# Depthwise and omni convolutions on 112-row tiles without a gap, band blocks packed, row sums taken channel by channel

## The chip, the cores and the metric

The kernel runs on one core of one Trainium2 chip. The metric is the device time of one execution in microseconds (us). Engines: PE is TensorE, with PEld for its weight loads; DVE is VectorE; ACT is ScalarE; POOL is GpSimd; SP only issues DMAs here, as ACT also does. Before the change, three runs gave 5991.86, 6002.13 and 6011.43 us, a median of 6002.13 us.

## The reference

The input x is 16 images of 192 channels of 56 by 56 pixels, float32. Two blocks follow each other.

```
# block 1
x_pw = bn(einsum('bchw,oc->bohw', x, pw_w)) + x
out  = bn(dwconv(x_pw, 13x13)) + bn(x_pw * dw1_w)
y    = gelu(out)                                  # erf form
# block 2, tok = y as tokens of 192 channels
xi   = omni(ln(tok) * ln1_g + ln1_b)              # a0*x + a1*dw1x1 + a2*dw3x3 + a3*dw5x5
k, v, r = xi @ wk.T, xi @ wv.T, sigmoid(xi @ wr.T)
v    = wkv along rows, then along columns         # two scans over 3136 tokens
tok += gamma1 * ((r * v) @ wo.T)
xf   = omni(ln(tok) * ln2_g + ln2_b)
tok += gamma2 * (sigmoid(xf @ wr.T) * (square(relu(xf @ wk.T)) @ wv.T))
```

What the change touches are the three depthwise convolutions (13x13 once, 5x5 twice) and the sums over channels that the layer norms need.

## The kernel before

`build` (L1658) runs blocks one after the other, with all engines meeting between them: `prepare` (weights), `pointwise` (the 1x1 convolution), `depthwise` (13x13), `norm_scales`, `omni` (5x5), `attention`, `norm_scales`, `omni`, `feed_forward`. Intermediate images go through scratch tensors in device memory. I call the three convolution blocks dw13, omni1 and omni2.

**How a depthwise convolution becomes matmuls.** A channel's 16 images are cut into 28 pairs of image rows. A pair of rows lies on the partitions: row 0 on partitions 0 to 55, row 1 above. A convolution over rows and columns is then a few products with banded matrices: for each distance d between the pair read and the pair written there is one band matrix, and the moving operand is all pairs of all images shifted by d (up to 16 x 28 = 448 columns). dw13 has d from -3 to 3, omni from -1 to 1. Each product is three matmuls (L87 to L89), since operands are split into a rounded high part and a rest: high x high, high x rest, rest x high. That makes 21 matmuls for a channel of dw13, 9 for a channel of omni.

**The gap.** The two rows of a pair stand at PITCH = 62 partitions from each other, with 6 zero partitions (56 to 61) between them in tiles of PXP = 118 partitions; PXC = 112 is the count without the gap. A channel's bands are a matrix with `cols` columns (862 for 13x13, 366 for 5x5) of which the product for d reads the 118 columns from 124 * (dmax ± d). In omni the first gap partition carries the layer norm's bias: its row of the bands is the "edge" row, and its row in the input is a constant (made from a row of -1 in the table of means, L775). In dw13 the input and the bands already use 112 partitions (`parts` = PXC), but outputs, and the bands' columns, still have the gap.

**dw13 (`depthwise`, L362).** Groups of 8 channels, 24 groups, two buffers. For each channel:
- ACT rounds the bands (L529, 112x862) and the input, which it turns from image order into pair order (L531); it does so 3 channels ahead, into 4 slots
- POOL subtracts: rest of the bands (L418), rest of the input (L488)
- PE does the 21 matmuls; ACT applies Gelu with a bias from PSUM into the group's output (L545)

After a group's 8 channels DVE makes the sums for the layer norm: it sums the 8 channels (`tensor_reduce`, L507), adds to the running sum (L509), squares the group (L510), sums (L512) and adds (L514). SP loads the input and bands of the group after next (L430, L441); ACT stores the group (L548). At the start DVE clears both band tiles (L495) before SP may load.

**omni (L561).** The same, with these differences: DVE scales the input by the table of inverse deviations (L681, 4 channels at a time), writing it in pair order, then subtracts the table of means (L687); both tables lie in PSUM. DVE also makes the rest of the bands (L693), POOL the rest of the input (L661), ACT the two roundings (L721, L723) and the copy out of PSUM (L734). At the start DVE clears four whole tiles (L667, L668). The loads of the group after next are issued by SP when the input has been scaled, and when the last band of the group has been split. `copy_pairs` (L118) makes every load and store that crosses the gap of two DMAs of 56 partitions:

```
    for r in range(2):
        tile, rest = slice(r * PITCH, r * PITCH + W), r * W
```

`norm_scales` (L751) turns the sums into the two tables; its last step is a DMA that writes the row of -1.

Of the kernel before, what the change touches and what calls it, by code (L numbers as in the profile page):

```python
# [117 lines left out]
def copy_pairs(eng, to, of, signal):  # L118


    for r in range(2):
        tile, rest = slice(r * PITCH, r * PITCH + W), r * W
        part = []
        for ap in (to, of):
            dims = [list(d) for d in ap.ap]
            if dims[0][1] == PXP:
                part.append(ap[tile])
            else:
                part.append(bass.AP(ap.tensor, ap.offset + rest * dims[0][0], [[dims[0][0], W]] + dims[1:]))
        eng.dma_start(part[0], part[1]).then_inc(signal, 16)  # L130
# [231 lines left out]
def depthwise(nc, B, name, src, parts, k, f_d, dst, bias_d, stats, flipped=False):  # L362

    dmax, centre, length, cols = band(k)
    N = B * PJ
    assert N <= 512
    with ExitStack() as ctx:
        m = Mem(nc, ctx)
        wt = [m.sb(f"{name}_band{u}", [PXP, G, cols]) for u in range(2)]
        raw = [m.sb(f"{name}_in{u}", [PXP, B, G, PJ]) for u in range(2)]
        z = raw
        out = [m.sb(f"{name}_out{u}", [PXP, B, G, PJ]) for u in range(2)]  # L380
# [9 lines left out]
        zeroed = m.sem(f"{name}_bands_zeroed")  # L390
# [5 lines left out]
        out_read = m.sem(f"{name}_output_summed")  # L396
        sq = m.sb(f"{name}_squares", [PXP, B, G, PJ])
        part = [m.sb(f"{name}_part{n}", [PXP, B, PJ]) for n in range(2)]
        reduced = m.sem(f"{name}_group_reduced")
        summed = m.sem(f"{name}_sums_updated")  # L400
        block = ctx.enter_context(nc.Block())
        flat = lambda t: t[:, :, :].rearrange("p a b -> p (a b)")
        by_pair = lambda ap: ap.rearrange("p b j -> p j b")
        IN = 32
        BASE = 2 * G
        step_in = PITCH if parts == PXP else W
# [6 lines left out]

        def rest_of_band(eng, i, n):
            u, cc, _, _ = channel(i, n)
            p = [q[0:parts, :] for q in wp[n % SLOTS]]
            eng.wait_ge(rounded_done, i * (4 * G) + (2 * n + 1))
            eng.tensor_tensor(rounded(p[1]), wt[u][0:parts, cc, :], p[0], ALU.subtract).then_inc(band_split, 1)  # L418

        @block.sync  # L420
        def _(sp):
# [1334 lines left out]
```

## Time and profile before

| | us |
|---|---|
| runs, median of 3 | 6002.13 |
| the profiled execution, its own time | 6008.11 |
| its span in the profile | 6006.3 |
| PE busy | 4937.5 |
| DVE busy | 4211.5 |
| ACT busy | 3702.6 |
| POOL busy | 3425.7 |

The profiled execution has 6 us over the median. The granted clock of PE has a mean of 0.929. Busy PE counts pipelined matmuls in full, so a busy PE isn't PE at its peak. Stages, from the first and last instruction of each: dw13 runs from about 379 to 1213, omni1 from 1222 to about 1690, omni2 from 3737 to about 4190, with the attention in between and the feed-forward behind.

### The profile page before, as it was taken

To read this page: it belongs to the slowest core of one execution; us is meant where nothing else is said; L and a number is where in the kernel's file an instruction comes from. 1 tells how busy PE (TensorE), PEld (TensorE's weight loads), DVE (VectorE), ACT (ScalarE), POOL (GpSimd) and SP (SyncE) were. 2 spreads that over 40 slices of the span, in tenths; PEclk is the share of its full clock that TensorE was granted. 3 is DMA by queue.
4 is the path that set the end of the run, shared out by engine and by line. 5 is a ranking of instruction groups with operands and counts; after the bars stand their busy time and mean duration, and the time that the engine had idled before them with its cause. 6 is when DMAs were issued, how large, how long until landed. Compare 5 with 4: busy or idle time off the path is not lost. (4 is left out here: it accounts for less than half of the span.)

```text
span 6006.3 us, 77285 instructions
## 1 busy us (share of the span) xinstructions
PE 4937.5 (82%) x23504; PEld 3954.3 (66%) x23504; DVE 4211.5 (70%) x5193; ACT 3702.6 (62%) x6950; POOL 3425.7 (57%) x2796
## 2 busy tenths in 40 slices
PE   5969999958866766767667673788899999999999
PEld 5969999847632443433334332676788888888888
DVE  4427777789849898888888885897555555555555
ACT  0016666545557888888888884565565665656565
POOL 0019999835549687777777872454444444444444
PEclk9979999979988988888889886999999999999999
DMA  6977777578840223213212122887422322322320
GB/s 170 264 187 197 193 196 205 148 185 255 245 104 11 68 52 76 65 43 88 54 44 65 44 65 56 233 268 226 105 69 54 82 60 56 86 56 54 88 54 24
DMA packets 389868, 689.60 MB, mean 115 GB/s; under 512 B 22399, under 2 KB 347986, under 8 KB 370194
## 3 DMA queue, kind: packets, MB, share of 16 engines
q1 hardware_dynamic: 335184, 529.89, 36.6%
q10 hardware_dynamic: 54386, 156.21, 7.3%
q8 instruction: 130, 2.13, 0.2%
q14 instruction: 168, 1.38, 0.1%
HBM read 452.17 MB, written 233.87 MB: 114 GB/s over the span
## 5 line engine op out<-in xcount | busy, mean ns | idle before, releaser
L1543 POOL TENSOR_TENSOR hidden_part<-hidden_whole,hidden_part 128x448 fp32r<-128x448 f32 x672 | 751.5, 1154 | 1025.9 <-ACT hidden_part L1508 1025.7
L661 POOL TENSOR_TENSOR omni_in_part<-omni_norm,omni_in_part 118x448 fp32r<-118x448 f32 x384 | 466.0, 1215 | 555.5 <-ACT omni_in_part L723 539.7
L1412 PE MATMUL f_out_ps<-hidden_part,ffn_wv_parts 128*128 128x448 f32 (+1 forms) x3360 | 720.8, 370 | 0.7 <-POOL hidden_part L1543 0.7
L418 POOL TENSOR_TENSOR dw_band_part<-dw_band,dw_band_part 112x862 fp32r<-112x862 f32 x192 | 438.7, 2285 | 470.6 <-ACT dw_band_part L529 470.5
L1412 PEld LDWEIGHTS f_out_ps<-hidden_part,ffn_wv_parts 128*128 128x128 f32 (+1 forms) x3360 | 578.1, 177 | 103.7 <-POOL hidden_part L1543 35.1
L87 PE MATMUL omni_ps<-omni_in_part,omni_band_part 118*118 118x432 f32 (+1 forms) x1152 | 435.7, 378 | 236.2 <-DVE omni_band_part L693 218.4
L1217 POOL TENSOR_TENSOR input_times_v<-input_factor,v_all 128x448 f32<-128x448 f32 x336 | 419.6, 1249 | 362.8 <-ACT input_factor L1110 343.3
L1586 DVE TENSOR_SCALAR hidden_whole<-f_hid_ps 128x448 f32<-128x448 f32 x672 | 417.6, 622 | 250.5 <-POOL hidden_part L1543 155.9
L1039 PE MATMUL proj_ps<-mixT_low,kvr_weights_low 128*128 128x448 f32 x672 | 354.0, 611 | 203.9 <-ACT k_all L1101 174.1
L87 PE MATMUL dw_ps<-dw_in_part,dw_band_part 112*118 112x432 f32 (+3 forms) x1344 | 473.7, 352 | 57.4 <-POOL dw_in_part L488 57.4
L1041 PE MATMUL proj_ps<-mixT_ends,kvr_weights_ends 128*128 128x448 f32 x1008 | 515.3, 595 | 0.0
L89 PE MATMUL dw_ps<-dw_in_part,dw_band_part 112*118 112x432 f32 (+3 forms) x1344 | 476.4, 354 | 0.0
L88 PE MATMUL dw_ps<-dw_in_part,dw_band_part 112*118 112x432 f32 (+3 forms) x1344 | 474.0, 353 | 0.0
L529 ACT ACTIVATE dw_band_part<-dw_band 112x862 fp32r<-112x862 f32 x192 | 176.2, 918 | 411.9 <-DMA dw_band<-flat 398.4
L89 PE MATMUL omni_ps<-omni_in_part,omni_band_part 118*118 118x432 f32 (+1 forms) x1152 | 419.5, 364 | 0.0
L88 PE MATMUL omni_ps<-omni_in_part,omni_band_part 118*118 118x432 f32 (+1 forms) x1152 | 418.9, 364 | 0.0
L1224 POOL TENSOR_TENSOR v_all<-input_times_v,input_factor 128x448 f32<-128x448 f32 x336 | 385.0, 1146 | 58.1 <-ACT input_factor L1126 55.7
L87 PEld LDWEIGHTS omni_ps<-omni_in_part,omni_band_part 118*118 118x118 f32 x1152 | 209.0, 181 | 312.0 <-DVE omni_band_part L693 270.9
L1055 PE MATMUL out_ps<-attention_out_weights,r_all 128*112 128x193 f32 x896 | 246.0, 359 | 200.5 <-DVE residual_pairs L1302 170.3
L1508 ACT ACTIVATE hidden_part<-hidden_whole 128x448 fp32r<-128x448 f32 x672 | 388.9, 579 | 21.3
L1412 PE MATMUL f_hid_ps<-ffn_mixT_part,ffn_wk_high 128*128 128x448 f32 x1344 | 396.2, 376 | 5.3 <-DVE hidden_whole L1586 5.3
L721 ACT ACTIVATE omni_band_part<-omni_band 118x366 fp32r<-118x366 f32 x384 | 194.0, 505 | 304.6 <-DMA omni_band<-edge_att 148.9
(183 smaller groups left out, 13650.6 us busy)
## 6 DMA issues: line engine op xcount, KB each, us to landing
dw_band<-flat SPq DMA_DIRECT2D x48, 1508.5 KB
xin<-x SPq DMA_DIRECT2D x16, 2352.0 KB, 13.1
x_pointwise<-xp ACTq DMA_DIRECT2D x16, 2352.0 KB, 18.9
dw_in<-x_pointwise SPq DMA_DIRECT2D x24, 1568.0 KB
y_gelu<-dw_out ACTq DMA_DIRECT2D x48, 784.0 KB
omni_in<-y_gelu SPq DMA_DIRECT2D x48, 784.0 KB
att_mix<-omni_out ACTq DMA_DIRECT2D x48, 784.0 KB
residual_pairs<-y_gelu SPq DMA_DIRECT2D x16, 2352.0 KB, 11.9
```

The costliest lines, as they stand in the source:

```text
L87: pe.matmul(bank, w_hi, x_hi, start=start, stop=False)
L88: pe.matmul(bank, w_hi, x_lo, start=False, stop=False)
L89: return pe.matmul(bank, w_lo, x_hi, start=False, stop=stop)
L418: eng.tensor_tensor(rounded(p[1]), wt[u][0:parts, cc, :], p[0], ALU.subtract).then_inc(band_split, 1)
L661: pool.tensor_tensor(rounded(p[1][:, :, :]), z[u][:, cc], p[0][:, :, :], ALU.subtract).then_inc(in_split, 1)
L1041: pe.matmul(to[:, 0:TC], keep.w_end[:, o, part * 128:(part + 1) * 128], x_end[:, t, :], start=False, stop=True).then_inc(bank_ready, 1)
L1217: pool.tensor_tensor(grid(EV[unit.slot % 2]), grid(E[unit.slot]), part_of(vS, unit), ALU.mult).then_inc(ev_done, 1)
L1224: pool.tensor_tensor(part_of(vS, unit), grid(EV[unit.slot % 2]), grid(E[unit.slot]), ALU.mult).then_inc(wkv_done, 1)
L1412: return pe.matmul(bank, rounded(w), rounded(x), start=start, stop=stop)
L1508: act.activation(rounded(kk[n % 2][0][:, h, :]), whole[h % KW][:, :], ACT.Copy).then_inc(kh_ready, 1)
L1543: pool.tensor_tensor(rounded(kk[n % 2][1][:, h, :]), whole[h % KW][:, :], kk[n % 2][0][:, h, :], ALU.subtract).then_inc(kl_ready, 1)
L1586: dve.tensor_scalar_max(whole[h % KW][:, :], hidden_bank(n, h)[:, 0:TC], 0.0).then_inc(relu_done, 1)
```

## The change

- Tiles of the three convolutions have 112 partitions, the two rows next to each other, and outputs have no gap. Matmuls of dw13 go from 118 to 112 output rows, those of omni from 118 x 118 to 113 x 112.
- The band tiles in memory keep their 862 and 366 columns, but the parts are packed: `band_blocks` reads 14 blocks (dw13) or 6 (omni) of 56 columns at a pitch of 62, so that a part has 784 or 336 columns.
- `load_band_rows` doesn't load the 56 columns or the 62 that are always zero for a row of the pair; POOL clears these margins, once. The whole-tile memsets are gone. dw13's loads wait for POOL's four memsets; omni's first input doesn't wait at all.
- Loads and stores of images are one DMA of 112 partitions in place of two of 56. Band loads are still two of 56.
- dw13's sums are made by channel: square, add to the sum, add the square to its sum, all three on DVE for every channel, in place of two reduces, a square and two adds for a group.
- omni keeps its input in image order from the load to the matmul. The parts have one zero pair ahead and one behind each image, so that a shift by d is a shift of the window: all 9 matmuls have 448 columns, read as 16 pieces of 28. The bias row is partition 112, set to 1 by a DMA of ones.
- `norm_scales` no longer writes the row of -1, and its memsets and paired DMAs are gone.

```
+def band_blocks(ap, count):
+    return free(ap, [[PITCH, count], [1, W]])
+def blocks(ap):
+    return ap.rearrange("p (n w) -> p n w", w=W)
+def load_band_rows(eng, wt, f_d, at, length, cols, signal):
+    for r, (lo, hi) in enumerate(((PITCH, cols), (0, cols - W))):
+        eng.dma_start(wt[r * W:(r + 1) * W, :, lo:hi],
+                      dram(f_d, at + (PITCH * r + lo), [[1, W], [length, G], [1, hi - lo]])).then_inc(signal, 16)
...
 depthwise, PE
-                        at = 2 * PITCH * (dmax - d if flipped else dmax + d)
-                        mm = split_matmul(pe, ps[cc][0:PXP, lo * B:hi * B],
+                        at = PXC * (dmax - d)
+                        mm = split_matmul(pe, ps[cc][0:PXC, lo * B:hi * B],
...
 depthwise, POOL
+            for u in range(2):
+                for margin in (slice(0, PITCH), slice(cols - W, cols)):
+                    pool.memset(wt[u][:, :, margin], 0.0).then_inc(zeroed, 1)
...
-                    rest_of_band(pool, i, n)
+                    p = wp[n % SLOTS]
+                    pool.wait_ge(rounded_done, i * (4 * G) + (2 * n + 1))
+                    pool.tensor_tensor(rounded(blocks(p[1][:, :])), band_blocks(wt[u][:, cc, :], BLOCKS),
+                                       blocks(p[0][:, :]), ALU.subtract).then_inc(band_split, 1)
...
 depthwise, DVE
-                dve.memset(wt[u][:, :, :], 0.0).then_inc(zeroed, 1)
...
-                    dve.tensor_reduce(part[0][:, :, :], by_pixel(out[u]), AX_X, ALU.add).then_inc(reduced, 1)
-                    dve.tensor_add(s1[:, :], s1[:, :], flat(part[0])).then_inc(summed, 1)
-                    dve.tensor_mul(sq[:, :, :, :], out[u][:, :, :, :], out[u][:, :, :, :]).then_inc(out_read, 1)
-                    dve.tensor_reduce(part[1][:, :, :], by_pixel(sq), AX_X, ALU.add).then_inc(reduced, 1)
-                    dve.tensor_add(s2[:, :], s2[:, :], flat(part[1])).then_inc(summed, 1)
+                for n in range(2 * G):
+                    u, cc, number, _ = channel(i, n)
+                    o = out[u][:, :, cc, :]
+                    dve.wait_ge(ps_free, number + G)
+                    dve.wait_ge(squares_summed, number)
+                    dve.tensor_mul(sq[:, :, :], o, o).then_inc(squared, 1)
+                    dve.wait_ge(summed, number + G)
+                    dve.tensor_add(s1, s1, o).then_inc(summed, 1)
+                    dve.wait_ge(squared, number + (G + 1))
+                    dve.tensor_add(s2, s2, sq[:, :, :]).then_inc(squares_summed, 1)
...
 depthwise and omni, ACT, at a group's end
-                        copy_pairs(act, pair_group(dst, B, i * 2 + u),
-                                   out[u][:, :, :, :].rearrange("p b c j -> p (b c j)"), stored[u])
+                        act.dma_start(pair_group(dst, B, i * 2 + u),
+                                      out[u][:, :, :, :].rearrange("p b c j -> p (b c j)")).then_inc(stored[u], 16)
...
 omni
+        z = [m.sb(f"{name}_norm{u}", [ROWS, B, G, PJ]) for u in range(2)]
+        wp = [[m.sb(f"{name}_band{s}_part{n}", [ROWS, BLOCKS * W]) for n in range(2)] for s in range(SLOTS)]
+        zp = [[m.sb(f"{name}_in{s}_part{n}", [ROWS, B, 1 + PJ + 1]) for n in range(2)] for s in range(SLOTS)]
...
 omni, SP
+            load_input(place(0), 0)
+            for u in range(2):
+                sp.dma_start(z[u][PXC:ROWS, :, :, :].rearrange("p b c j -> p (b c j)"), ones
+                             ).then_inc(ones_loaded, 16)
             sp.wait_ge(zeroed, 4)
-            for u in range(2):
-                load_input(place(u), u)
-                load_bands(place(u), u)
+            load_bands(place(0), 0)
+            load_input(place(1), 1)
+            load_bands(place(1), 1)
...
 omni, PE
-                        mm = split_matmul(pe, ps[n % NB][0:PXP, lo * B:hi * B],
-                                          [x[:, at:at + PXP] for x in wp[n % SLOTS]],
-                                          [flat(x)[:, (lo + d) * B:(hi + d) * B] for x in zp[n % SLOTS]],
+                        at = PXC * (dmax + d)
+                        mm = split_matmul(pe, by_image(ps[n % NB][0:PXC, 0:N]),
+                                          [x[:, at:at + PXC] for x in wp[n % SLOTS]],
+                                          [x[:, :, 1 + d:1 + d + PJ] for x in zp[n % SLOTS]],
...
 omni, POOL: margins as in depthwise, and the pads of the parts
+            for s in range(SLOTS):
+                for x in zp[s]:
+                    pool.memset(x[:, :, :], 0.0).then_inc(padded, 1)
...
 omni, DVE
-                dve.memset(wt[u][:, :, :], 0.0).then_inc(zeroed, 1)
-                dve.memset(raw[u][:, :, :, :], 0.0).then_inc(zeroed, 1)
...
-                dve.tensor_mul(by_image(z[u][:, part]), raw[u][:, :, part, :], free(rs_ps, [[PJ, B], [0, H], [1, PJ]])
-                               ).then_inc(scaled, 1)
+                dve.tensor_mul(z[u][0:PXC, :, part, :], raw[u][:, :, part, :], of_table(rs_ps)).then_inc(scaled, 1)
...
 norm_scales, SP
-            sp.wait_ge(step, 5)
-            sp.dma_start(s1[W:W + 1, :], minus_one).then_inc(gap_set, 16)
-            sp.wait_ge(gap_set, 16)
```

## Rows read from the trace of the kernel before

**Rows 1.** Busy time of each engine by stretch: pointwise, dw13, omni1, omni2; (x) instructions, then PE clock, DMA share, GB/s.
```profile
120.00:240.00 120.00, 120.00 (x740) 120.00 (x739) 51.22 (x92) 0.00 (x0) 0.00 (x0) 1.00 1.01 268
...
800.00:1200.00 400.00, 394.20 (x2070) 369.56 (x2069) 294.51 (x63) 244.45 (x300) 361.54 (x194) 1.00 0.68 180
...
1295.00:1691.00 396.00, 334.77 (x1572) 278.16 (x1570) 339.17 (x256) 235.40 (x520) 213.05 (x173) 0.99 0.85 241
...
3790.00:4190.00 400.00, 349.50 (x1656) 292.87 (x1656) 356.95 (x272) 252.55 (x547) 217.62 (x182) 1.00 0.85 250
```

**Rows 2.** Timeline of ACT in omni1, two copies out of PSUM that each waited for PE.
```profile
1441.91 0.55 ACT L734 ACTIVATE omni_out<-omni_ps 118x448 f32<-118x448 f32 x1 [0.38 <-PE omni_ps L89]
...
1443.70 0.55 ACT L734 ACTIVATE omni_out<-omni_ps 118x448 f32<-118x448 f32 x1 [0.38 <-PE omni_ps L89]
```

**Rows 3.** Waits from 1295 to 1691: engine, line, waited for, us in total, times, longest.
```profile
ACT omni_band_part L721 <- DMA omni_band<-edge_att: 108.3, 20, 7.4
```

**Rows 4.** Groups of instructions, DVE in omni1 and omni2.
```profile
L681 DVE TENSOR_TENSOR omni_norm<-omni_in,omni_scales 118x1792 f32<-118x1792 f32 x96 | 318.0, 3315 | 23.9 <-issue 20.1 <-DMA omni_in<-y_gelu 2.4 <-DMA omni_in<-tok 1.3
...
L693 DVE TENSOR_TENSOR omni_band_part<-omni_band,omni_band_part 118x366 fp32r<-118x366 f32 x384 | 295.7, 789 | 83.3 <-ACT omni_band_part L721 82.8
...
L687 DVE TENSOR_TENSOR omni_norm<-omni_norm,omni_scales 118x1792 f32<-118x1792 f32 x96 | 192.9, 2011 | 0.0
```

**Rows 5.** DMA queues from 1300 to 1690: packets, MB, share of 16 engines.
```profile
q1 hardware_dynamic: 21445, 58.70, 61.0%
q10 hardware_dynamic: 3064, 35.10, 24.2%
```

**Rows 6.** Timeline from the end of dw13 to the first matmul of omni1.
```profile
1194.90 0.77 ACTq L130 DMA_DIRECT2D y_gelu<-dw_out  x2
...
1212.54 0.62 DVE L514 TENSOR_TENSOR y_square_sum<-y_square_sum,dw_part 118x448 f32<-118x448 f32 x1
...
1222.24 2.50 DVE L667 MEMSET omni_band<- 118x2928 f32 x1 [2.35 <-PEq L637]
...
1235.31 0.77 SPq L130 DMA_DIRECT2D omni_in<-y_gelu  x2
...
1246.40 6.14 DVE L681 TENSOR_TENSOR omni_norm<-omni_in,omni_scales 118x1792 f32<-118x1792 f32 x2 [10.08 <-issue]
...
1257.76 0.72 PE L87 MATMUL omni_ps<-omni_in_part,omni_band_part 118*118 118x448 f32 x1 [63.56 <-DVE omni_band_part L693]
```

**Rows 7.** Timeline at the start of dw13.
```profile
378.87 5.80 DVE L495 MEMSET dw_band<- 118x6896 f32 x1 [12.32 <-issue]
386.06 5.80 DVE L495 MEMSET dw_band<- 118x6896 f32 x1 [1.39 <-issue]
...
418.92 0.92 ACT L529 ACTIVATE dw_band_part<-dw_band 112x862 fp32r<-112x862 f32 x1 [398.40 <-DMA dw_band<-flat]
```

**Rows 8.** Groups of instructions, POOL in dw13: busy us, mean ns, idle before.
```profile
L418 POOL TENSOR_TENSOR dw_band_part<-dw_band,dw_band_part 112x862 fp32r<-112x862 f32 x192 | 438.7, 2285 | 470.6 <-ACT dw_band_part L529 470.5
...
L488 POOL TENSOR_TENSOR dw_in_part<-dw_in,dw_in_part 112x448 fp32r<-112x448 f32 x192 | 292.4, 1523 | 0.0
```

**Rows 9.** Timeline of DVE and POOL in dw13: start us, duration us, instruction.
```profile
705.48 0.90 DVE L514 TENSOR_TENSOR y_square_sum<-y_square_sum,dw_part 118x448 f32<-118x448 f32 x1
...
727.38 3.88 DVE L510 TENSOR_TENSOR dw_squares<-dw_out 118x3584 f32<-118x3584 f32 x1
...
705.86 1.79 POOL L488 TENSOR_TENSOR dw_in_part<-dw_in,dw_in_part 112x448 fp32r<-112x448 f32 x1
707.60 2.08 POOL L418 TENSOR_TENSOR dw_band_part<-dw_band,dw_band_part 112x862 fp32r<-112x862 f32 x1
709.62 1.42 POOL L488 TENSOR_TENSOR dw_in_part<-dw_in,dw_in_part 112x448 fp32r<-112x448 f32 x1
710.99 1.73 POOL L418 TENSOR_TENSOR dw_band_part<-dw_band,dw_band_part 112x862 fp32r<-112x862 f32 x1
...
727.77 5.41 POOL L418 TENSOR_TENSOR dw_band_part<-dw_band,dw_band_part 112x862 fp32r<-112x862 f32 x1 [0.80 <-ACT dw_band_part L529]
```

More of the change, by code:

```diff
@@ L557, in _, with omni @@
             for u in range(2):
-                act.wait_ge(stored[u], 32 * (NG // 2 + 1))
-def omni(nc, B, name, src, f_d, s_d, dst, rs, ms):
+                act.wait_ge(stored[u], 16 * (NG // 2 + 1))
+def omni(nc, B, name, src, f_d, s_d, ones, dst, rs, ms):
     dmax, _, length, cols = band(K5)
+    BLOCKS = 2 * (2 * dmax + 1)
     N = B * PJ
+    ROWS = PXC + 1
     assert N <= 512
@@ L595, in omni @@
         BASE = 2 * G
-        W_LOADS, IN_LOADS = 48, 32
-        flat = lambda t: t[:, :, :].rearrange("p j b -> p (j b)")
+        W_LOADS, IN_LOADS = 48, 16
+        by_image = lambda ap: ap.rearrange("p (b j) -> p b j", j=PJ)
+        inner = lambda t: t[:, :, 1:1 + PJ]
+        of_table = lambda ap: free(ap, [[PJ, B], [0, H], [1, PJ]])
         def channel(i, n):
@@ L655, in _ @@
         def _(pool):
+            for u in range(2):
+                for margin in (slice(0, PITCH), slice(cols - W, cols)):
+                    pool.memset(wt[u][0:PXC, :, margin], 0.0).then_inc(zeroed, 1)
+            for s in range(SLOTS):
+                for x in zp[s]:
+                    pool.memset(x[:, :, :], 0.0).then_inc(padded, 1)
+            pool.wait_ge(padded, 2 * SLOTS)
             with pool.Fori(0, NG // 2) as i:
@@ L802, in _ @@
             act.activation(s2[:, :], s2[:, :], ACT.Sqrt).then_inc(root, 1)
-def transposed(bank, reverse=False):
-    s = -1 if reverse else 1
-    return free(bank[0:CT, :], [[PXP, JC], [s * PITCH, 2], [s, W]], PXP - 1 if reverse else 0)
 def turned(bank, rows):
@@ L1685, in build @@
                 mi = Mem(nc, inner)
-                s1, s2 = mi.sb("y_sum", [PXP, B * PJ]), mi.sb("y_square_sum", [PXP, B * PJ])
-                depthwise(nc, B, "dw13", xpw_d, PXC, K13, f13_d, y_d, bias_d, (s1, s2), flipped=True)
-                norm_scales(nc, "ln1", s1, s2, ins["minus_one"], kept_d=sy_d)
-                omni(nc, B, "omni1", y_d, f5a_d, sa_d, mixa_d, s2, s1)
+                s1, s2 = mi.sb("y_sum", [PXC, B * PJ]), mi.sb("y_square_sum", [PXC, B * PJ])
+                depthwise(nc, B, "dw13", xpw_d, K13, f13_d, y_d, bias_d, (s1, s2))
+                norm_scales(nc, "ln1", s1, s2, kept_d=sy_d)
+                omni(nc, B, "omni1", y_d, f5a_d, sa_d, ins["ones"], mixa_d, s2, s1)
             attention(nc, B, keep, mixa_d, y_d, sy_d, tok_d, s1_d, s2_d)
@@ L1692, in build @@
                 mi = Mem(nc, inner)
-                s1, s2 = mi.sb("t_sum", [PXP, B * PJ]), mi.sb("t_square_sum", [PXP, B * PJ])
-                norm_scales(nc, "ln2", s1, s2, ins["minus_one"], s1_d, s2_d)
-                omni(nc, B, "omni2", tok_d, f5f_d, sf_d, mixf_d, s2, s1)
+                s1, s2 = mi.sb("t_sum", [PXC, B * PJ]), mi.sb("t_square_sum", [PXC, B * PJ])
+                norm_scales(nc, "ln2", s1, s2, s1_d, s2_d)
+                omni(nc, B, "omni2", tok_d, f5f_d, sf_d, ins["ones"], mixf_d, s2, s1)
         feed_forward(nc, B, ins, keep, mixf_d, tok_d, out)
@@ L1730, in layout @@
         "ident": np.eye(PXP, dtype=np.float32),
-        "minus_one": np.full((1, x.shape[0] * PJ), -1.0, np.float32),
+        "ones": np.ones((1, x.shape[0] * G * PJ), np.float32),
         "pw_wt": t(l0("pw_w")),
```

197 lines of the change are left out of this document (77 added, 120 removed).

## The prediction

> **What bounds the kernel now.** I read the busy times by stage first [rows 1], since a mean over the span mixes stages. In dw13 PE issues without a pause: 2070 matmuls in 394.2 us of work, so a channel's 21 take 4.00 us. POOL is busy 361.5 of 400 us there, the second limit and not far off. In both omni stages PE is busy 85 to 87%, DVE 86 to 89%, and the DMA share stands at 0.85, whereas in the pointwise stage it reached 1.01. A channel takes 396 / 1572 x 9 = 2.27 us in omni1 and 400 / 1656 x 9 = 2.17 us in omni2, so a group of 8 takes 18.1 and 17.4 us. Where PE is fed, two channels follow each other in 1443.70 - 1441.91 = 1.79 us, 14.3 us for a group [rows 2]. So omni waits. The waits say for what: ACT stood 108 us of 396 waiting for bands to land, at 20 group starts [rows 3]. DVE is no better placed: 8 x 0.789 + 2 x 3.315 + 2 x 2.011 = 17.0 us for a group [rows 4], some of it waiting that the durations hold.
>
> Why 0.85 is a full DMA: per group of omni the output is 1.61 MB, the input the same, the bands 1.31 MB. From 1300 to 1690 the output queue used 24.2% of 16 x 390 us for 35.1 MB = 21.9 groups, 69 engine-us each; the other queue 61.0% for 58.7 MB, 20.0 groups, 190 each, of which 69 are input and 121 bands [rows 5]. The sum 259 over 16 engines is 16.2 us, over 14 it is 18.5, and the measured period is 18.1. Pointwise has transfers of 96 and 112 partitions and a share near 1; omni's large ones all have 56, and 0.85 is near 14/16 [rows 1]. I take it that a 56-partition transfer uses 14 engines. The Trainium skill ("DMA: Bandwidth & Descriptors", why a DMA increments its semaphore by 16) says that the number of engines is the largest up to 16 that divides the slowest dimension, 14 for 56 and 16 for 112; the share agrees.
>
> **omni, steady state.** Bytes: bands shrink from 366 to 304 and 310 columns, 0.839 of before, 121 to 102 engine-us. Images move on 16 engines instead of 14; bands stay at 56 rows. Busiest engines: (69 + 69) / 16 + 102 / 14 = 15.9 us, against 18.5 by the same sum before. PE: now 9 x 448 = 4032 columns where it had 3936, so 1.79 becomes 1.83 us, 14.7 for a group. DVE: L681 wrote pair order at 3.3 us; in image order it should cost what L687 does, 2.0, so 8 x 0.79 + 4 x 2.01 = 14.4. ACT and POOL keep their work, in pieces of 28 elements. The slowest of these is the DMA at 15.9, where its model read 18.5 for a measured 18.1 and 17.4; I take 15.8 for both. Gain: 24 x (18.1 - 15.8) + 24 x (17.4 - 15.8) = 93 us. At best PE bounds: 24 x (3.4 + 2.7) = 146. If engines aren't what limits and only the bytes count (239.5 / 259 = 0.925), 24 x (1.4 + 1.3) = 65.
>
> **omni, start.** DVE's four memsets stand between 1222.24 and the first load at 1235.31; the first matmul comes at 1257.76 [rows 6]. Now the first load goes out at once, and the row of -1, whose transfer shows as 2.35 us idle ahead of 1222.24, is gone, so at about 1220.3. Landing takes at most the 11.1 us from 1235.31 to 1246.40, and from the first scaling to the first matmul it was 11.4 us, now 2 x 1.3 less: first matmul at 1220.3 + 11.1 + 8.8 = 1240.2, a gain of 17.6. POOL's 12 memsets (448 to 496 columns) are not in the trace: as fast as DVE's 5.80 us for 6896 columns [rows 7] they take 0.4 us each, at POOL's 1.52 us for 448 [rows 8] some 1.6. Even then, 19 us in all, ACT starts at 1240 and the gain is 14. I take 18 for each omni, 36 together.
>
> **dw13, start.** Two memsets hold the loads back from 378.87 to 391.86 [rows 7]. Four of POOL's, 1.6 to 6.5 us by the same two prices, take their place; 3 is nearest to a memset's own price. That is 10 us, and of the 27.1 us until 418.92 the bands, 6.8% fewer bytes, give 1. Gain 11.
>
> **dw13, end.** After the last Gelu DVE works from 1194.9 to 1213.16 [rows 6]. With sums by channel three operations of 0.62 us are left, and the stage ends with the last store, issued at 1194.90: 69 / 16 = 4.3 us of transfer and some us of latency, about 1202. Gain 11 (8 to 16).
>
> **dw13, steady state: the price of the change.** PE's work doesn't shrink: output rows of a matmul are not its columns. But DVE now makes 3 operations a channel, each with both inputs in SBUF, beside POOL's two. The timeline shows what that costs [rows 9]: L510 ran from 727.38 to 731.26, and POOL's L418, issued at 727.77, took 5.41 us where it takes 2.08 or 1.73 alone. L514 beside L488 made it 1.79 instead of 1.42: 0.37 us lost to POOL for one operation of 448 columns. POOL alone needs 3.39 us for a channel (707.60 to 710.99) at the slower of its two band times and 0.35 less at the other, 3.2 on average; with 784 columns instead of 862 (9% of 1.9) 3.05. Adding 3 x 0.37 gives 4.16 us against PE's 4.00: POOL and DVE together become the limit, by 0.16 x 192 = 31 us. DVE itself isn't late: ACT waits for its sums only when an output buffer comes round, 8 channels later. PE's waits on the new limit are short, so its clock should stay at 1.00.
> Bounds: below nothing, since PE's 4.00 doesn't move. Above, POOL loses the 0.62 us that an add takes alone [rows 6]: 3.05 + 1.86 = 4.91. Or its band subtraction in 14 pieces runs at the per-element time of L488, which reads transposed: 1.42 x 784 / 448 = 2.48 in place of 1.73, again 4.91 with 0.37. Either is 175 us. I take 31, as L418 stays contiguous in runs of 56 and the 0.37 is measured.
> The Trainium skill ("SBUF — State Buffer", the engine ports) says that a DVE operation with two SBUF inputs and a POOL operation reading SBUF exclude each other for the whole instruction. The row of L510 agrees; that of L514 shows less than the whole, 0.37 of 0.62. By the page's rule the stage would take 4.91 us a channel.
>
> **Sum.** -11 - 11 + 31 - 36 - 93 = -120 us. Everything else (pointwise, attention, feed-forward) is untouched. The profiled execution took 6008.1 us, so 5888; it has 6 over the median of 6002.1, against which it is 5882.
>
> **Rivals.**
> - *The port doesn't bind* (0.20): what DVE takes falls into POOL's idle tenth, the channel stays at 4.00: 31 us more gained, 5851. For it speaks that durations on POOL are rough; against it, that POOL is busy nine tenths already.
> - *omni stays where it is* (0.12): the rate at which bands and images come isn't set by engines or bytes, and DVE's gain is hidden behind it. -120 + 93 = -27, 5975. Against it: at equal bytes the model gives the period within 7%.
> - *Whole exclusion in dw13* (0.12), the slower end: every add holds POOL for 0.62 us, 4.91 us a channel, +175 in place of +31: +24, 6026. It decides from 0.88 us a channel on, since the rest gives 151 and slower means 18 us. For it the stretch of L418, against it that of L514.
> - *The shifted windows don't do what they say* (0.04): PE reads 28-column pieces at half the rate. Then a channel of omni takes 3.67 us, a group 29.4: 24 x (11.3 + 12.0) = 559 slower, not 93 faster, about 6530. No row shows a matmul that reads in pieces, so nothing but the contiguous rate speaks against it.
>
> **Numbers.** The forecast has 0.52. About 0.3% (18 us) is what a measurement can tell from no change. Forecast, free port and three quarters of the flat omni are faster: 0.81. Slower: the whole exclusion up to its milder part, and the slow windows: 0.13. The rest, 0.06, is no change. Range: the low end has the free port and nearly PE's bound in omni, -11 - 11 - 36 - 146 = -204, about 5805; the high end takes in the flat omni with some more of the port's price, 5990.
>
> **What would show it.** Right: L418 near 1.7 to 2.1 us when undisturbed, PE in dw13 with short waits for POOL at 4.1 to 4.2 us a channel, DVE's adds often over 1 us; L681 at 2.0; DMA share in omni up, the wait for bands down, a group at 15.8; first matmul of omni some 20 us after the norm. Wrong: dw13's channel over 4.5 or at 4.00; L681 still at 3.3; omni's matmuls longer at a clock of 1.00; omni's group over 17.

## The result, and the profile after

The changed kernel takes 5950.9 us (median of 4, 5947.2 to 5954.1) against 5997.0 of the kernel before on the same chip (median of 4, 5991.2 to 6011.4): a ratio of 0.992, 95% interval 0.9906 to 0.9933. It is 46 us faster where 120 were forecast. The profiled executions have spans of 5948.0 and 6006.3 us, 58.3 apart; the stages below are read from these two. "Norm" is the block `norm_scales`.

| stretch | before | after | difference | forecast |
|---|---|---|---|---|
| dw13, first matmul at | 423.4 | 407.0 | -16 | -11 |
| dw13, first to last matmul | 770.5 | 828.1 | +58 | +31 |
| dw13, last Gelu to norm | 19.3 | 17.9 | -1 | -11 |
| omni1 and omni2, norm to first matmul | 44.3, 47.8 | 26.0, 29.2 | -37 | -36 |
| omni1, first matmul to last store's issue | 430.4 | 395.0 | -35 | -55 |
| omni2, the same | 417.4 | 398.1 | -19 | -38 |

The starts came nearly as forecast. Two things did not: dw13 lost nearly twice what was set for it and gave almost nothing back at its end, and omni's steady state gained little more than half.

**dw13.** The stretch of [rows 1] and, under it, what ACT waited for from 407 to 1330 (engine, line, waited for: us in total, times, longest):
```profile
800.00:1200.00 400.00, 376.59 (x1901) 340.71 (x1900) 393.77 (x271) 220.01 (x283) 347.50 (x183) 0.96 0.64 168
```
```profile
ACT dw_out L526 <- PE dw_ps L89: 190.3, 112, 3.4
ACT dw_out L526 <- DVE y_sum L494: 86.9, 11, 10.3
ACT L526 <- DVE y_sum L494: 69.6, 8, 8.7
```
DVE went from 295 to 394 us of 400: it is the engine that is hardly ever idle, and ACT's first Gelu of a group (L526), which writes an output buffer, waited 156 us for its sums. The forecast had looked for PE waiting on POOL. The timeline of DVE and POOL shows how, in the stretch of [rows 9]:
```profile
698.21 2.12 POOL L470 TENSOR_TENSOR dw_band_part<-dw_band,dw_band_part 112x784 fp32r<-112x784 f32 x1
698.65 2.16 DVE L494 TENSOR_TENSOR y_sum<-y_sum,dw_out 112x448 f32<-112x448 f32 x1
700.29 1.79 POOL L474 TENSOR_TENSOR dw_in_part<-dw_in,dw_in_part 112x448 fp32r<-112x448 f32 x1
700.73 1.84 DVE L496 TENSOR_TENSOR y_square_sum<-y_square_sum,dw_squares 112x448 f32<-112x448 f32 x1
702.04 2.12 POOL L470 TENSOR_TENSOR dw_band_part<-dw_band,dw_band_part 112x784 fp32r<-112x784 f32 x1
702.68 1.97 DVE L492 TENSOR_TENSOR dw_squares<-dw_out 112x448 f32<-112x448 f32 x1
...
719.06 0.62 DVE L494 TENSOR_TENSOR y_sum<-y_sum,dw_out 112x448 f32<-112x448 f32 x1
719.60 0.62 DVE L496 TENSOR_TENSOR y_square_sum<-y_square_sum,dw_squares 112x448 f32<-112x448 f32 x1
719.85 0.64 ACT L526 ACTIVATE dw_out<-dw_ps,dw_cols 112x448 f32<-112x448 f32 x1 [8.30 <-DVE y_sum L494]
721.31 2.25 POOL L470 TENSOR_TENSOR dw_band_part<-dw_band,dw_band_part 112x784 fp32r<-112x784 f32 x1 [3.92 <-ACT dw_band_part L511]
```
In the first six lines one DVE start stands between each two POOL starts; over the whole stage that holds for 341 of the 354 pairs of POOL operations that follow each other without a pause. POOL's operations are 0.40 longer than alone (2.12 for 1.72, 1.79 for some 1.40; the values alone are e3's, below), so it gets through a channel in 702.04 - 698.21 = 3.83 us, faster than PE's 4.00. DVE gets two turns in that time and needs three. It falls behind by most of an operation a channel, until ACT stands still at a group's start, POOL runs dry (3.92 us), and DVE catches up at 719.60 - 719.06 = 0.54 us each.

**omni.** Stretches in both omni stages, columns as in [rows 1]; then PE's matmuls on either kernel's tile (ns, least/median/most), before first; then DVE's and POOL's groups in omni1.
```profile
1316.00:1596.00 280.00, 268.18 (x1226) 213.98 (x1225) 206.59 (x205) 182.78 (x410) 215.81 (x136) 1.00 0.98 263
3760.00:4040.00 280.00, 266.86 (x1219) 212.66 (x1218) 204.63 (x202) 179.30 (x403) 213.71 (x135) 1.00 0.97 262
```
```profile
L87 PE MATMUL omni_ps<-omni_in_part,omni_band_part x1152: 353/362/724, 1257.8 to 4187.4; 118*118 118x448 f32 x192
```
```profile
L87 PE MATMUL omni_ps<-omni_in_part,omni_band_part x1152: 373/377/684, 1279.3 to 4135.2; 113*112 113x448 f32 x192
```
```profile
L655 POOL TENSOR_TENSOR omni_in_part<-omni_norm,omni_in_part 113x448 fp32r<-113x448 f32 x192 | 298.9, 1567 | 104.4 <-ACT omni_in_part L714 102.9
...
L681 DVE TENSOR_TENSOR omni_band_part<-omni_band,omni_band_part 113x336 fp32r<-113x336 f32 x191 | 112.6, 591 | 99.2 <-ACT omni_band_part L711 99.0
L670 DVE TENSOR_TENSOR omni_norm<-omni_in,omni_scales 112x1792 f32<-112x1792 f32 x46 | 92.6, 2013 | 4.4 <-DMA omni_in<-y_gelu 4.3
```
The scaling fell to 2.01 us as forecast [rows 4]. The DMA share is 0.98 and 0.97, where before had 0.89 in the same two stretches (0.85 over the whole stages), which looks as if more engines took part, as forecast; yet the rate rose by 4 to 5% only, to 262 and 263 GB/s from before's 253 and 250 (before's second stretch begins 11 us ahead of omni2's first matmul):
```profile
1316.00:1596.00 280.00, 237.26 (x1108) 196.54 (x1107) 251.26 (x187) 164.69 (x364) 149.14 (x122) 0.99 0.89 253
3760.00:4040.00 280.00, 233.76 (x1091) 195.57 (x1092) 254.01 (x188) 169.15 (x369) 148.50 (x124) 0.96 0.89 250
```
A group takes 395.0 / 24 = 16.5 us, and ACT still waited for bands 79.5 us in omni1. Matmuls of 448 columns in pieces of 28 follow each other every 0.215 us (e6, below), where the forecast had 0.203.

### The profile page after: what moved, and what is told of

Its sections match the earlier page's. It is cut to its first block and busy times, and to the rows that moved or that the text cites. A ratio compares the mean times of both kernels' runs of the same rounds, so it can differ in the third digit from the quotient of the medians.

```text
span 5948.0 us, 77644 instructions
## 1 busy us (share of the span) xinstructions
PE 4981.9 (84%) x23504; PEld 3940.7 (66%) x23504; DVE 4253.6 (72%) x5637; ACT 3670.0 (62%) x6950; POOL 3588.9 (60%) x2824
## 5 line engine op out<-in xcount | busy, mean ns | idle before, releaser
L655 POOL TENSOR_TENSOR omni_in_part<-omni_norm,omni_in_part 113x448 fp32r<-113x448 f32 x384 | 602.9, 1581 | 206.8 <-ACT omni_in_part L714 204.1
L1564 DVE TENSOR_SCALAR hidden_whole<-f_hid_ps 128x448 f32<-128x448 f32 x672 | 417.4, 622 | 250.0 <-POOL hidden_part L1521 157.4
L87 PE MATMUL dw_ps<-dw_in_part,dw_band_part 112*112 112x432 f32 (+3 forms) x1344 | 484.5, 361 | 77.9 <-POOL dw_in_part L474 41.3
L87 PE MATMUL omni_ps<-omni_in_part,omni_band_part 113*112 113x448 f32 x1152 | 439.7, 382 | 118.7 <-POOL omni_in_part L655 87.9
L88 PE MATMUL dw_ps<-dw_in_part,dw_band_part 112*112 112x432 f32 (+3 forms) x1344 | 483.2, 360 | 0.0
L89 PE MATMUL dw_ps<-dw_in_part,dw_band_part 112*112 112x432 f32 (+3 forms) x1344 | 479.7, 357 | 0.0
L470 POOL TENSOR_TENSOR dw_band_part<-dw_band,dw_band_part 112x784 fp32r<-112x784 f32 x192 | 400.6, 2087 | 123.5 <-ACT dw_band_part L511 122.8
L88 PE MATMUL omni_ps<-omni_in_part,omni_band_part 113*112 113x448 f32 x1152 | 437.4, 380 | 0.0
L89 PE MATMUL omni_ps<-omni_in_part,omni_band_part 113*112 113x448 f32 x1152 | 437.0, 379 | 0.0
L511 ACT ACTIVATE dw_band_part<-dw_band 112x784 fp32r<-112x784 f32 x192 | 164.5, 857 | 390.1 <-DMA dw_band<-flat 382.4
L1484 ACT ACTIVATE hidden_whole<-hidden_whole 128x448 f32<-128x448 f32 x672 | 379.2, 564 | 0.9 <-DVE hidden_whole L1564 0.3
L1019 PEld LDWEIGHTS proj_ps<-mixT_ends,kvr_weights_ends 128*128 128x128 f32 x1008 | 192.9, 205 | 270.3 <-issue 270.3
```

Of the source, the lines that this page charges most:

```text
L87: pe.matmul(bank, w_hi, x_hi, start=start, stop=False)
L88: pe.matmul(bank, w_hi, x_lo, start=False, stop=False)
L89: return pe.matmul(bank, w_lo, x_hi, start=False, stop=stop)
L470: pool.tensor_tensor(rounded(blocks(p[1][:, :])), band_blocks(wt[u][:, cc, :], BLOCKS), blocks(p[0][:, :]), ALU.subtract).then_inc(band_sp ...
L655: pool.tensor_tensor(rounded(inner(p[1])), z[u][:, :, cc, :], inner(p[0]), ALU.subtract).then_inc(in_split, 1)
L1019: pe.matmul(to[:, 0:TC], keep.w_end[:, o, part * 128:(part + 1) * 128], x_end[:, t, :], start=False, stop=True).then_inc(bank_ready, 1)
```

## The experiments

Theory for dw13 (**turns**): while both have work, DVE gets one operation for each of POOL's; what doesn't fit runs when POOL is idle, at 0.54 us each. With k DVE operations a channel, a channel takes 3.83 + 0.54 (k - 2), at least PE's 4.00. Rivals: each DVE operation simply adds its 0.40 us to POOL's 3.12 (3.12 + 0.40 k, "port time" in the texts below); DVE holds POOL for its whole 0.62 us; the gapless tiles themselves are slower. The texts of e1 and e2 give the sum of port times as the theory and the whole 0.62 as its rival; turns as a formula came out of their results, so its agreement with them below was no forecast, and e10 is its only test ahead of a result. All times are from the first to the last matmul of dw13 unless said. Runs before e11 are single ones beside 5995.7 (e1 to e4), 5998.4 (e5 to e8) and 5999.4 (e9, e10; a median of nine) of the kernel before.

**e1, two operations a channel.**
```diff
-                    dve.tensor_add(s2, s2, sq[:, :, :]).then_inc(squares_summed, 1)
```


> The changed kernel with the add into s2 left out (the sums of squares stay 0): DVE has two operations a channel in dw13 instead of three. After took 828 us from dw13's first to its last matmul, 4.31 a channel. Theory (port time adds up): POOL's two subtractions take 3.12 us alone (1.72 + 1.40), each DVE operation with two SBUF inputs adds 0.40, a channel takes max(4.00, 3.12 + 0.40 k), so 4.00 for k = 2 (3.92 is hidden behind PE), the stretch 774 us, the kernel about 54 us shorter than after, and ACT no longer waits for DVE's sums. Rival 1 (DVE holds POOL for its whole 0.62 us): 3.12 + 1.24 = 4.36, no change. Rival 2 (PE or ACT is slower on the gapless tiles, the sums have no part in it): 4.31, no change.

5878.1 us; 767.7, 4.00 a channel. ACT waited for no sum, the norm began 8.1 us after the last Gelu instead of 17.9.

**e2, four operations.**
```diff
+                    dve.tensor_add(extra[:, :, :], sq[:, :, :], sq[:, :, :]).then_inc(extra_done, 1)
```


> The changed kernel with one more DVE operation a channel in dw13, sq + sq into a tile that nobody reads: four instead of three. Theory (port time adds up): 3.12 + 4 x 0.40 = 4.72 us a channel, 906 us from first to last matmul, 78 more than after. Rival 1 (whole 0.62 us each): 0.62 more a channel, 4.93, 119 us more. Rival 2 (the sums have no part in it): 4.31, no change.

6055.5 us; 927.6, and 24.2 us from the last Gelu to the norm. DVE and POOL, the same view as above:
```profile
1289.72 1.79 POOL L476 TENSOR_TENSOR dw_in_part<-dw_in,dw_in_part 112x448 fp32r<-112x448 f32 x1
1290.16 1.83 DVE L500 TENSOR_TENSOR y_square_sum<-y_square_sum,dw_squares 112x448 f32<-112x448 f32 x1
1291.46 2.13 POOL L472 TENSOR_TENSOR dw_band_part<-dw_band,dw_band_part 112x784 fp32r<-112x784 f32 x1
1291.91 2.16 DVE L502 TENSOR_TENSOR dw_extra<-dw_squares 112x448 f32<-112x448 f32 x1
...
1295.27 2.15 POOL L472 TENSOR_TENSOR dw_band_part<-dw_band,dw_band_part 112x784 fp32r<-112x784 f32 x1
```
POOL still needs 1295.27 - 1291.46 = 3.81 us a channel: the fourth operation costs POOL nothing while both run. Counting what the end of the stage takes over e1's 8.1 us to the stretch, a channel takes (828.1 + 9.8) / 192 = 4.36 us with three operations and (927.6 + 16.1) / 192 = 4.92 with four; turns give 4.37 and 4.91. Added port times give 4.32 and 4.72, and the whole 0.62 us gives 4.98 and 5.60. The sum of port times falls by e2 alone, the whole 0.62 us by both, and slower tiles by e1's 4.00.

**e3, the sums in PSUM.** Four banks for the convolution instead of eight, two for the sums.
```diff
-            s1, s2 = [by_image(s[:, :]) for s in stats]
+            s1, s2 = [by_image(s[0:PXC, 0:N]) for s in sums]
...
+            for total, s in zip(sums, stats):
+                dve.tensor_copy(s[:, :], total[0:PXC, 0:N]).then_inc(kept, 1)
```


> The changed kernel with the two sums of dw13 kept in two PSUM banks (the convolution has four banks instead of eight) and copied to SBUF at the end: of DVE's three operations a channel only the square reads two tiles from SBUF. Theory (only two-input SBUF operations take POOL's time): 3.12 + 0.40 = 3.52, hidden behind PE: 4.00 a channel, 774 us; DVE keeps up, so the norm begins 8 to 10 us after the last Gelu instead of 17.9; 54 + 8 = 62 us shorter than after. Rival (adds with one input in PSUM stretch POOL as well, as the scaling in omni seems to): 4.31, no change. Rival 2 (four banks are too few): PE waits on bank_free, over 4.00 without POOL being busy.

5883.6 us; 768.8, and 8.0 us to the norm. Groups of dw13:
```profile
L473 POOL TENSOR_TENSOR dw_band_part<-dw_band,dw_band_part 112x784 fp32r<-112x784 f32 x191 | 342.6, 1794 | 153.2 <-ACT dw_band_part L519 153.0
L477 POOL TENSOR_TENSOR dw_in_part<-dw_in,dw_in_part 112x448 fp32r<-112x448 f32 x191 | 272.5, 1427 | 0.0
...
L495 DVE TENSOR_TENSOR dw_squares<-dw_out 112x448 f32<-112x448 f32 x192 | 148.2, 772 | 447.2 <-ACT dw_out L534 447.2
L497 DVE TENSOR_TENSOR dw_sum<-dw_sum,dw_out 112x448 f32<-112x448 f32 x192 | 119.6, 623 | 0.0
```
The same add that took 1.56 us on the mean beside POOL (after's L494) takes 0.62 with its sum in PSUM, whatever POOL does, and POOL is back near its own 1.72 and 1.40. Four banks are enough.

**e4, sums by group on gapless tiles.** DVE's part of the kernel before, on 112 partitions.
```diff
-                    dve.tensor_add(s1, s1, o).then_inc(summed, 1)
...
+                    dve.tensor_reduce(part[0][:, :, :], by_pixel(out[u]), AX_X, ALU.add).then_inc(cleared, 1)
...
```


> The changed kernel with the sums of dw13 by group as before (a reduction over 8 channels, an add, a square, a reduction, an add), on 112 partitions. Theory: dw13 from first to last matmul back at 4.00 a channel, 774 us, 54 less than after, and the end of the stage takes some 19 us from the last Gelu to the norm. Rival 2 (the gapless tiles themselves slow dw13): stays at 4.31.

5895.2 us; 767.6, and 19.2 us to the norm. So the sums by channel are the whole loss in dw13: without them the rest of the change is worth 100 us (5995.7 - 5895.2, single runs). The same trace shows where the rule of turns ends. Here DVE's additions stand alone between long reductions, and two of the 48 got no turn as long as POOL had work; the longer one waited past seven POOL starts at 1.38 to 1.74 us each, until POOL paused for 0.98 us:
```profile
942.73 11.23 DVE L496 TENSOR_TENSOR y_square_sum<-y_square_sum,dw_part 112x448 f32<-112x448 f32 x1
942.91 1.40 POOL L475 TENSOR_TENSOR dw_in_part<-dw_in,dw_in_part 112x448 fp32r<-112x448 f32 x1
...
954.46 1.74 POOL L471 TENSOR_TENSOR dw_band_part<-dw_band,dw_band_part 112x784 fp32r<-112x784 f32 x1 [0.98 <-ACT dw_band_part L511]
```
In the kernel before ten of the 24 additions of L509 waited past two POOL starts in the same way, 4.9 us each. So one turn for each POOL operation is what the kernels with sums by channel show, no rule for every pair of streams; what decides who comes first is not shown.

**e5 to e8, omni.** What limits it: bytes, DMA engines, or PE's reading in pieces?
```diff
-                                  [x[:, :, 1 + d:1 + d + PJ] for x in zp[n % SLOTS]],
+                                  [x[:, :, :].rearrange("p b j -> p (b j)")[:, 1 + d:1 + d + N] for x in zp[n % SLOTS]],
```


> The changed kernel with omni's matmuls reading 448 neighbouring columns of the padded input tile instead of 16 pieces of 28 (this mixes pad columns into the convolution). After took 395.0 us (omni1) and 398.1 us (omni2) from the first matmul to the last store's issue, 16.5 a group; a matmul every 0.215 us where before had 0.203. If PE's reading in pieces is what costs: spacing 0.203, a channel 1.83 instead of 1.94, a group 0.9 us shorter, 20 us less in each omni. If the DMA ends last (4.22 MB a group at 262 GB/s, 16.1 us): spacing 0.203, but both stretches within 5 us of after. If the width of the output or the pads have no part in the spacing: 0.215 as in after.


```diff
-                    load_bands(at, u)
+                    load_few(at, u)
```


> The changed kernel with the band loads of omni from the third group on cut to 32 columns a channel (the rest of the tile keeps the bands of the first two groups): 0.13 MB a group instead of 1.11, 3.35 MB in all instead of 4.33, by the same number of transfers. If the DMA ends last in omni: the wait for bands goes and PE bounds, 8 x 1.94 = 15.5 us a group instead of 16.5, 374 us in each omni, 45 us less in all. If it is PE or the work of ACT, DVE and POOL around it that ends last: both stretches within 8 us of after's 395 and 398.

> Both edits at once: cut band loads and matmuls that read 448 neighbouring columns. If DMA ends last and PE's pieces come next: 8 x 1.83 = 14.7 us a group, 355 us in each omni, 20 less than with the cut loads alone and 80 less than after in all. If DVE ends last after the DMA (8 x 0.51 to 0.58 + 4 x 2.01 = 12.1 to 12.7 us of work) or POOL (8 x 1.58 = 12.6): neither reaches 14.7, so no change by them; a stretch that stays at 374 would say that they wait on each other.


```diff
-                sp.dma_start(raw[u][:, :, :, :].rearrange("p b c j -> p (b c j)"),
...
+                for h in range(2):
+                    sp.dma_start(raw[u][h * W:(h + 1) * W, :, :, :].rearrange("p b c j -> p (b c j)"),
...
```


> The changed kernel with omni's images loaded and stored by two transfers of 56 partitions each, as before, instead of one of 112. If the number of engines a transfer uses is the limit (the forecast's model): (69 + 69 + 102) / 14 = 17.1 us a group instead of 15.9, both omni stages 1.2 x 24 = 29 us longer, a DMA share of 0.87 instead of 0.98. If it is the rate at which bytes move (about 262 GB/s in all, whatever the engines): both within 8 us of after.

From the first matmul to the last store's issue, omni1 and omni2; the whole kernel: after 395.0 and 398.1; e5 400.7 and 394.8, 5954.0; e6 375.7 and 374.8, 5904.7; e7 359.9 and 363.2, 5879.3; e8 398.9 and 401.4, 5964.5. The stretch 1316 to 1596 of e5, e6, e7 and e8 in this order:
```profile
1316.00:1596.00 280.00, 259.40 (x1207) 214.10 (x1205) 202.26 (x201) 178.90 (x399) 205.07 (x134) 0.97 0.98 259
```
```profile
1316.00:1596.00 280.00, 280.00 (x1301) 229.04 (x1300) 214.04 (x217) 200.61 (x434) 241.67 (x144) 1.00 0.68 215
```
```profile
1316.00:1596.00 280.00, 279.95 (x1355) 235.23 (x1354) 232.22 (x227) 211.13 (x451) 265.02 (x151) 1.00 0.70 224
```
```profile
1316.00:1596.00 280.00, 267.24 (x1221) 212.76 (x1220) 205.01 (x201) 177.91 (x401) 212.58 (x135) 1.00 0.89 261
```
e8 is the test of the forecast's model: with halves of 56 partitions the share falls to 0.89, near the 14/16 that it assumed, but the rate stays at 261 GB/s and each stage grows by 4 us, not 29. e6 takes away nearly a quarter of the bytes with the same number of transfers: PE is then busy without a gap (280.00 of 280) at 280 / 1301 = 0.215 us a matmul, and both stages come out where PE's floor was put (374). e7 shows what the pieces cost once nothing hides them: 280 / 1355 = 0.207 us a matmul, 14 us a stage, where 20 were expected. e5 shows that they cost nothing as long as bytes end last; its 400.7, a little over the 5 us allowed, has a stretch at the lower of the two clock levels in it (1.2 GHz: granted clock 0.97 on the mean, matmuls every 0.37 us around 1452). The limit of the changed kernel is the rate at which bytes move, some 262 GB/s on the mean of this mix of loads and stores, whatever the share; PE at 15.5 us a group stands right behind it, POOL (265 of 280 in e7) next. No run puts the same question to the kernel before.

**e9, does one input in SBUF take a turn?** In omni POOL's L655 takes 1.06 us alone and about 2.4 beside the scaling, which has one input in PSUM.
```diff
+                    dve.tensor_add(extra[:, :, :], s2, sq[:, :, :]).then_inc(extra_done, 1)
```


> The kernel with dw13's sums in PSUM (e3) and a fourth DVE operation a channel: the PSUM sum of squares plus the squares in SBUF, written to an SBUF tile that nobody reads. It has one input in SBUF and its output there, as omni's scaling has, beside which POOL's subtractions were stretched from 1.07 to about 2.4 us. If only operations with two inputs in SBUF take POOL's time: POOL's means stay at e3's 1.79 and 1.43 us, its busy time from 800 to 1200 at 297 us, the new operation at 0.62 us. If one input and the output in SBUF are enough: one of POOL's two operations a channel is 0.4 us longer, its busy time about 335, the new operation over 1 us. In both cases 3.12 + 2 x 0.40 = 3.92 stays under PE's 4.00 and the stretch at 769 us.


```profile
L475 POOL TENSOR_TENSOR dw_band_part<-dw_band,dw_band_part 112x784 fp32r<-112x784 f32 x191 | 346.4, 1814 | 153.4 <-ACT dw_band_part L526 153.3
L479 POOL TENSOR_TENSOR dw_in_part<-dw_in,dw_in_part 112x448 fp32r<-112x448 f32 x192 | 269.3, 1403 | 0.0
...
L506 DVE TENSOR_TENSOR dw_extra<-dw_sum,dw_squares 112x448 f32<-112x448 f32 x191 | 119.3, 625 | 6.5
```
No: all three as in e3 (768.96 the stretch). The 23 us that the whole, 5906.9, is over e3's lie behind omni2, in a part that no edit touches: 1835 us from omni2's last store to the end, against 1813.

In omni it isn't the scaling (L670) by itself either. These lines of the changed kernel are the case that e9 started from; POOL's three operations stand in one line:
```profile
1449.29 7.46 POOL L655 TENSOR_TENSOR omni_in_part<-omni_norm,omni_in_part 113x448 fp32r<-113x448 f32 x3 [0.16 <-ACT omni_in_part L714]
1450.61 0.50 DVE L681 TENSOR_TENSOR omni_band_part<-omni_band,omni_band_part 113x336 fp32r<-113x336 f32 x1
1451.03 2.01 DVE L670 TENSOR_TENSOR omni_norm<-omni_in,omni_scales 112x1792 f32<-112x1792 f32 x1
1452.96 0.50 DVE L681 TENSOR_TENSOR omni_band_part<-omni_band,omni_band_part 113x336 fp32r<-113x336 f32 x1
```
Between the scalings stands L681, the rest of a band, with both inputs in SBUF. All 133 operations of L655 that took over 2.0 us end 0.93 to 0.95 us after the end of an L681, and the three that had no DVE operation but L670 beside them took 1.08. So POOL waits for the operation with two SBUF inputs. Why it is held while the one before that still runs (the 133 start 0.6 to 1.7 us before their L681) stays open, and so does why a scaling or centring followed by a band's rest leaves POOL's at 1.17 us on the median in the kernel before.

**e10, three turns.** POOL's band subtraction cut in two.
```diff
-                    pool.tensor_tensor(rounded(blocks(p[1][:, :])), band_blocks(wt[u][:, cc, :], BLOCKS),
+                    half = BLOCKS // 2
+                    pool.tensor_tensor(rounded(blocks(p[1][:, 0:half * W])), band_blocks(wt[u][:, cc, :], half),
...
```


> The changed kernel with POOL's band subtraction in dw13 cut in two of 7 blocks each: three POOL operations a channel beside DVE's three. Theory (DVE gets one operation for each of POOL's; two turns a channel are one too few, and the third runs only while POOL idles): now DVE has three turns and keeps up, ACT no longer waits for y_sum (156 us of waits in after), and POOL with 3 x 0.40 added to its 3.2 to 3.3 becomes the limit: 4.4 to 4.5 us a channel, 845 to 864 us from first to last matmul, PE waiting for POOL at every channel. Rival (it is the sum of port time alone, in whatever order): the third instruction's own cost, about 0.1 us a channel, comes on top, 847 us, and ACT goes on waiting for y_sum. Rival 2 (POOL's turns have no part in it): 828 as in after.


```profile
701.87 1.34 POOL L471 TENSOR_TENSOR dw_band_part<-dw_band,dw_band_part 112x392 fp32r<-112x392 f32 x1
702.42 1.26 DVE L496 TENSOR_TENSOR dw_squares<-dw_out 112x448 f32<-112x448 f32 x1
703.16 1.36 POOL L473 TENSOR_TENSOR dw_band_part<-dw_band,dw_band_part 112x392 fp32r<-112x392 f32 x1
703.61 1.40 DVE L498 TENSOR_TENSOR y_sum<-y_sum,dw_out 112x448 f32<-112x448 f32 x1
704.48 1.78 POOL L478 TENSOR_TENSOR dw_in_part<-dw_in,dw_in_part 112x448 fp32r<-112x448 f32 x1
704.93 1.81 DVE L500 TENSOR_TENSOR y_square_sum<-y_square_sum,dw_squares 112x448 f32<-112x448 f32 x1
706.22 1.35 POOL L471 TENSOR_TENSOR dw_band_part<-dw_band,dw_band_part 112x392 fp32r<-112x392 f32 x1
```
5946.2 us; 832.1, 4.33 a channel (706.22 - 701.87 = 4.35). As turns demand, the bottleneck changed hands: POOL is busy 299.8 of 300 us (800 to 1100), DVE keeps up, ACT waited for no sum, and the norm came 8.0 us after the last Gelu. The time was 13 us under the lower end of the expectation, as the halves, 0.94 us without DVE's 0.40, were cheaper than taken. The stretch alone, 832.1, is nearer to the 828 of the rival in which turns have no part; it is the waits that speak against both rivals.

**e11 and e12, the best version, timed in five rounds.** e12 is e3 again; e11 also holds back the second group's loads, in dw13 and in omni, and scales and centres omni's first group half by half.
```diff
+            sp.wait_ge(in_loaded[0], IN_LOADS)
+            sp.wait_ge(w_loaded[0], W_LOADS)
             load_input(place(1), 1)
...
-            for step in (scale, centre_):
-                for half in range(2):
+            for half in range(2):
+                for step in (scale, centre_):
```


> e3 (sums in PSUM) with three edits at the starts of stages: dw13 and both omni issue the second group's loads only when the first group's have landed, and omni's first group is scaled and centred half by half. Each start moves 4.4 MB (dw13) or 2.7 MB (omni) for the first group, 17 and 10 us at 262 GB/s, where in e3 the first ACT operation waits 25 and 17.4 us from the first load's issue. If the second group's transfers take part of the rate until then: first matmul of dw13 5 to 8 us earlier and of each omni 3 to 7, some 15 us in all, 5868. If transfers of one queue go in the order of their issue: the starts stay within 2 us, and dw13's or omni's second group may come late: 5880 to 5890.

> e3 once more, timed against the kernel before in rounds: the kernel that is ahead of both so far. Expected from its one look (5883.6 against 5995.7): a ratio of 0.981, 67 us less than the changed kernel.

e12: 5882.6 us (5877.1 to 5887.4), ratio 0.9798, interval 0.9776 to 0.982. e11: 5866.9 (5848.3 to 5875.3), ratio 0.9768, interval 0.9743 to 0.9792. Both beat before and after. The intervals of the two overlap, though no run of e11 was as long as the shortest of e12. The reason given for e11 fell: from the first load's issue to the first matmul dw13 takes 28.0 us (e12 29.0) and omni1 19.4 (19.5). Some 7 us of the 12 between the two spans lie in omni's steady state (395.2 and 395.7 against 400.4 and 397.7); why, I did not test.

## Why the prediction was wrong

The sign and the starts held, and the range (5805 to 5990) has the result in it; the size did not hold. By the table the stages gave 52 us, 68 less than the forecast's 120: 27 are missing in dw13's steady state, 10 at its end, 38 in omni's steady state, and the starts gave 6 more. (The spans differ by 6 more than the stages, the medians by 6 less.)

- **dw13, steady: "Adding 3 x 0.37 gives 4.16".** The price to POOL was nearly right (0.40 an operation, e2's rows). POOL's own time was 3.12, not 3.05, and above all the sum was made for POOL's side only. "DVE itself isn't late" is the step that failed: it looked at when the sums are due (8 channels later), not at whether DVE has time for them at all. In this stage DVE gets as many turns as POOL has operations, 2 in 3.83 us, and a buffer of 8 channels doesn't help against a steady deficit. By turns the term is (4.37 - 4.00) x 192 = 71 us, of which 10 fall into the tail; forecast 31, measured 58 and the tail's 10. The reading of L514 in [rows 9] gave the loss to the wrong engine alone: POOL lost 0.37, but DVE's own operations wait for a POOL operation to end.
- **Against the Trainium skill.** In the changed kernel's rows POOL's and DVE's starts alternate (341 of 354 pairs). The Trainium skill ("SBUF — State Buffer", the engine ports) says that the two exclude each other; by that rule as I costed it (the whole 0.62 us, 4.91 a channel) the stage would have been 115 us longer than measured. The rows agree with the exclusion: a DVE operation that starts beside a POOL operation ends some 0.5 us after it (698.65 + 2.16 against 698.21 + 2.12). But the price to POOL is 0.40 and not 0.62, and who waits for whom is what the costing lacked.
- **dw13, end: "three operations of 0.62 us are left".** True only for a DVE that keeps up. It had a backlog and worked until 1252.3 + 0.6; in e1, e3 and e10, where it keeps up, the norm comes 8.0 us after the last Gelu, which is the forecast's -11.
- **omni, steady: "I take it that a 56-partition transfer uses 14 engines" and the period 259 / 14 = 18.5.** The first half agrees with the shares (0.89 in e8, 0.98 after; no view shows single engines). The second is the step that failed here, as engine time isn't the limit: e8 costs 4 us a stage, not 29. By bytes a group is 3.21 MB of images and 1.32 MB of bands before, 1.11 now; 4.32 MB at 262 GB/s is 16.5 us, the measured period (no test, as the rate is read from the same stretch; e6 and e8 are the tests). The forecast had this case as its bound ("only the bytes count"), 65 us, of which 55 came. It was 65 because it was scaled by engine time (0.925); by bytes the ratio is 4.32 / 4.53 = 0.954, and 4.6% of omni2's 417 us are 19: measured 19. omni1 gained 16 more than that, because before it ran at 4.53 MB / 17.9 us = 253 GB/s; what held it there I did not find. DVE is a rival that no run tests: before, its work filled 17.0 of the 17.4 to 17.9 us of a group [rows 4], and the scaling's fall from 3.3 to 2.0 us relieved it, so part of the gain may be its.
- **Matmuls in pieces.** The rival's half rate was far off; they cost 4% (0.215 for 0.207 us, e6 and e7), hidden while bytes end last (e5).
- **Starts.** dw13 -16 for -11: POOL's four memsets took 1.79 us together, not 3, and the landing came sooner. omni -37 for -36.

## What to carry to other kernels

Where VectorE and GpSimd both work from SBUF, count turns as well as time. With both engines busy without a pause, VectorE got one two-input operation for each of GpSimd's here, so k operations beside m leave k - m that need idle time of GpSimd; a single one among others may wait longer (11.23 us in e4). Keep running sums in PSUM, and their part of the conflict is gone (e3: 67 us, for two banks and four fewer for the convolution). A DMA share near 1 names neither the limit nor its cure: compare GB/s across stages, then take bytes away in one run and engines in another.

## What the runs showed of the hardware that I had not expected

- A VectorE operation of 112x448 with both inputs in SBUF lasts 0.62 us alone, mostly 1.8 to 2.2 in the profile beside GpSimd's, and costs GpSimd 0.40 (e2's rows); shorter GpSimd operations, 1.34 us, give it its turn sooner (e10). Coming alone it can wait past seven GpSimd operations, 11.23 us, that lose nothing by it (e4).
- With one input in PSUM, output in PSUM or in SBUF, it lasts 0.62 us beside a busy GpSimd and costs it nothing (e3, e9). In omni GpSimd is stretched from 1.06 to some 2.4 us where an operation with two SBUF inputs follows such a one: it is held until that has run, and ends 0.94 us after it.
- With images in transfers of 112 partitions at a DMA share of 0.98, or of 56 at 0.89, the DMA moves the same 261 to 263 GB/s (after, e8).
- A matmul of 448 columns read in pieces of 28 follows its forerunner after 0.215 us, contiguous after 0.207 (e6, e7).
